# Attention and a routed FFN in one launch: routing counts ahead of the scores, weight halves and the last attention groups moved at the seam

## Reference

```python
qkv = xn @ w_attn.T                      # 16 heads of 16
# per batch row, in chunks of 128 tokens, q and k through elu(.) + 1:
scores = where(mask, q_c @ k_c.T, 0)
num = scores @ v_c + q_c @ S;  den = scores.sum(-1) + q_c @ z
S += k_c.T @ v_c;  z += k_c.sum(axis=chunk)
attn = (num / (den + 1e-6)) @ w_proj.T
# ffn: 8 experts of 256 -> 1024 -> 256, one per token
top = argmax(xn @ gate_w.T + gate_b + expert_bias)
ffn = relu(xn @ w1[top] + b1[top]) @ w2[top] + b2[top]
```

## Time and profile before

| | us |
|---|---|
| median of 3 runs | 522.24 |
| those runs | 522.82, 519.31, 522.24 |
| the profiled execution: its own time | 518.55 |
| its span, first to last instruction | 516.8 |
| TensorE, VectorE, ScalarE, GpSimd busy | 486.6, 397.0, 278.9, 303.5 |
| mean granted TensorE clock | 0.986 |

### The profile page before, as it was taken

How to read it: one execution, slowest core, us unless ns; L and a number is a source line. 1 busy time by engine, 2 the same in 40 slices (tenths; PEclk the granted TensorE clock), 3 DMA queues, 4 the chain that set the end, 5 groups by cost and what they waited for, 6 DMA issues and landing times.

```text
span 516.8 us, 17902 instructions
## 1 busy us (share of the span) xinstructions
PE 486.6 (94%) x6265; PEld 402.2 (78%) x6265; DVE 397.0 (77%) x851; ACT 278.9 (54%) x536; POOL 303.5 (59%) x498
## 2 busy tenths in 40 slices
PE   7699999999999999999977869999999999999996
PEld 6578887888878887888865658888888888888884
DVE  3678898988889888897889537777776776776775
ACT  3447888788787787877763313323323333333330
POOL 5666889879888888888753273344344344343122
PEclk9989999999999999999997989999999999999999
DMA  8715667686676676766530462221222222200000
GB/s 258 248 53 146 203 196 212 189 237 193 185 224 182 210 208 197 211 189 194 173 128 22 153 171 76 64 78 59 69 68 66 77 63 63 70 23 27 22 17 1
DMA packets 39059, 67.50 MB, mean 131 GB/s; under 512 B 6237, under 2 KB 14686, under 8 KB 38848
## 3 DMA queue, kind: packets, MB, share of 16 engines
q1 hardware_dynamic: 33840, 53.37, 33.5%
q0 software_dynamic: 5136, 12.99, 8.4%
HBM read 51.39 MB, written 17.69 MB: 134 GB/s over the span
## 4 chain that ended last, share of the span: by engine, by line
PE 85%; DVE 5%; issue 4%; POOL 2%; DMA 2%; ACT 1%; DVEq 0%; POOLq 0%; ACTq 0%
PE ps L682 20%; PE ps L695 19%; PE ps L424 8%; PE ps L466 6%; PE ps L495 6%; PE ps L539 5%; PE ps L479 5%; PE ps L442 4%; PE ps L509 3%; PE ps L525 3%; PE ps L647 2%; PE ps L449 1%; PE ps L531 1%; PE ps L407 1%; DVE AR L785 1%
## 5 line engine op out<-in xcount | busy, mean ns | idle before, releaser
L682 PEld LDWEIGHTS ps<-AR,W 128*128 x1872 | 131.2, 98 | 41.1 <-issue 2.0
L682 PE MATMUL ps<-AR,W 128*128 128x128 f16 x1872 | 155.8, 220 | 0.9 <-ACT AR L1264 0.9
L695 PE MATMUL ps<-W,ST 128*128 x624 | 151.4, 328 | 0.0
L1273 ACT ACTIVATE ST<-ST 128x512 f16<-128x512 f32 x78 | 49.2, 630 | 117.1 <-DVE ST L1080 117.1
L1080 DVE SCALAR_TENSOR_TENSOR ST<-ps,TAs,B1S 128x512 f32<-128x512 f32 x78 | 58.6, 751 | 48.5 <-PE ps L682 48.4
L1433 POOL DMA_INDIRECT out<-AR x39 | 39.6, 1015 | 94.7 <-DVE AR L1112 90.8
L1370 POOL TENSOR_TENSOR W<-ST,W 128x512 f16<-128x512 f32 x64 | 74.3, 1161 | 19.2 <-ACT W L1199 18.3
L785 DVE TENSOR_TENSOR AR<-ps,CT 128x512 f32<-128x512 f32 x128 | 81.9, 683 | 2.4 <-PE ps L466 2.2
L1428 POOL DMA_INDIRECT XR<-scr,AR x39 | 44.4, 1139 | 48.7 <-DVE AR L1100 25.4
L1092 DVE SCALAR_TENSOR_TENSOR ST<-ST 128x512 f16<-128x512 f32 x78 | 53.6, 687 | 14.9 <-ACT ST L1273 14.9
L424 PE MATMUL ps<-xT,WA 128*128 128x128 f16 x768 | 49.1, 221 | 3.4 <-ACT xT L1148 3.4
(11 more groups left out here) (149 smaller groups left out, 789.9 us busy)
## 6 DMA issues: line engine op xcount, KB each, us to landing
ST<-in_w SPq DMA_DIRECT2D x128, 256.0 KB, 4.4
scr<-XR SPq DMA_DIRECT2D x32, 256.0 KB, 2.2
XR<-in_x SPq DMA_DIRECT2D x32, 128.0 KB, 4.7
scr<-XR SPq DMA_DIRECT2D x32, 128.0 KB, 4.6
AR<-in_b SPq DMA_DIRECT2D x1, 1024.0 KB, 5.2
AR<-in_wall SPq DMA_DIRECT2D x2, 388.0 KB, 3.9
XR<-scr,AR POOLq DMA_INDIRECT x40, 3.6
out<-AR POOLq DMA_INDIRECT x39, 2.5
```

The lines of the kernel that those rows point to most:

```text
L682: a = e.matmul(dst, W[:, off:off + 57472][:, bass.ds(place_of(s), 128)], XT16[s % 2][:, xl * 256 + k * 128:xl * 256 + (k + 1) * 128], star ...
L695: a = e.matmul(PS[4 + s % 2][:, 0:w], src[h % 4][:, fs], W[:, off:off + 57344 + w][:, bass.ds(place_of(s), w)], start=(f == 0 and w == 512 ...
L1273: e.activation(HH[h % 4], H32[h % 2], ACT.Relu).then_inc(a_hh, 1)
```

## The change

Six edits at the seam; nothing is computed otherwise. A new semaphore v_kt marks that first_slots has written KT.

1. TensorE: place(3) goes ahead of scores(30).
2. GpSimd: km(31), and with it all w_lo behind it, waits for v_kt. w_lo(63) goes ahead of gather_x16(0).
3. VectorE: the three ids operations and the whole computation of the slots' experts go ahead of s_mask(30); to_slots(1) no longer waits for a count of its own engine; res(30) goes ahead of y(31).
4. ScalarE: seven splits in one piece ahead of y1(30).
5. TensorE: yt2(30), pr(30) and yt1(31) go into slot 0 (behind tx(0), steps 0 and 1); yt2(31) and pr(31) move from steps 3 and 5 to 4 and 6.
6. VectorE: res(31) goes behind low(0). ScalarE: y2(31) goes behind tx(1).

```diff
@@ -293,8 +293,8 @@
         v_mx, t_mx, v_mm, t_mxa, v_sc, v_ffn = (sem(n) for n in ("v_mx", "t_mx", "v_mm", "t_mxa", "v_sc", "v_ffn"))
 
         p_tt, p_carry, v_ro, p_pl = (sem(n) for n in ("p_tt", "p_carry", "v_ro", "p_pl"))
-        v_o16, v_ox, t_rk, v_own, v_es, v_eq, v_ao, t_ids, v_ids, d_c16 = (
-            sem(n) for n in ("v_o16", "v_ox", "t_rk", "v_own", "v_es", "v_eq", "v_ao", "t_ids", "v_ids", "d_c16"))
+        v_o16, v_ox, t_rk, v_own, v_es, v_kt, v_eq, v_ao, t_ids, v_ids, d_c16 = (
+            sem(n) for n in ("v_o16", "v_ox", "t_rk", "v_own", "v_es", "v_kt", "v_eq", "v_ao", "t_ids", "v_ids", "d_c16"))
 
         v_rb, t_tx, a_tx, v_out, t_g2 = (sem(f"f_{n}") for n in ("rb", "ptx", "tx", "out", "g2"))
 
@@ -609,9 +609,9 @@
                     e.transpose(PBX, BM[:, :], ID32).then_inc(t_bmx, 1)
 
 
+            place(3)
             scores(NC - 2)
             st(NC - 2)
-            place(3)
             inter(NC - 2)
             warm(70)
 
@@ -631,9 +631,6 @@
             e.wait_ge(S["t32"], n_state(NC - 2))
             inter(NC - 1)
             pv(NC - 1)
-            yt2(NC - 2)
-            pr(NC - 2)
-            yt1(NC - 1)
 
             def tx(s):
 
@@ -702,6 +699,7 @@
             e.wait_ge(v_es, 1)
             expert(0)
             tx(0)
+            yt2(NC - 2)
             for t in range(8 * NS + LAG):
                 s, f = t // 8, t % 8
                 if s < NS:
@@ -710,9 +708,13 @@
                         tx(s + 1)
                     if f == 4 and s + 1 < NS:
                         expert(s + 1)
-                if t == 3:
+                if t == 0:
+                    pr(NC - 2)
+                if t == 1:
+                    yt1(NC - 1)
+                if t == 4:
                     yt2(NC - 1)
-                if t == 5:
+                if t == 6:
                     pr(NC - 1)
                 if t >= LAG:
                     g2((t - LAG) // 8, (t - LAG) % 8)
@@ -974,12 +976,12 @@
                 e.tensor_reduce(OB, RB8, X_AX, ALU.add).then_inc(dv.up(), 1)
                 e.wait_ge(dv.sem, dv.n)
                 e.wait_ge(p_pl, 3)
-                e.tensor_tensor(KT, KS, OB, ALU.add).then_inc(dv.up(), 1)
+                e.tensor_tensor(KT, KS, OB, ALU.add).then_inc(v_kt, 1)
+                e.wait_ge(v_kt, 1)
 
             def to_slots(i):
 
                 c = slice(16 * i, 16 * i + 16)
-                e.wait_ge(dv.sem, dv.n)
                 e.tensor_tensor(EQS[:, :, c], SLX[:, :, c], bm(KT[:, c], NS), ALU.is_equal).then_inc(dv.up(), 1)
                 e.wait_ge(dv.sem, dv.n)
                 e.tensor_tensor(EQS[:, :, c], EQS[:, :, c], bm(IDX[:, c], NS), ALU.mult).then_inc(v_eq, 1)
@@ -1030,8 +1032,11 @@
             to_slots(1)
             places(2)
             places(3)
-            s_mask(NC - 2, 0)
-            s_mask(NC - 2, 1)
+            e.tensor_tensor(GE, bc(cc(C_SL, 5 * NP), 7), bm(CSF[:, 0:7], 5 * NP), ALU.is_ge).then_inc(dv.up(), 1)
+            e.wait_ge(dv.sem, dv.n)
+            e.tensor_reduce(ESF, GE, X_AX, ALU.add).then_inc(dv.up(), 1)
+            e.wait_ge(dv.sem, dv.n)
+            e.tensor_tensor(ESP, ESF, cc(C_PK, 5 * NP), ALU.mult).then_inc(dv.up(), 1)
             e.wait_ge(t_ids, 1)
             pid = PS[1][:, 0:NS]
             e.tensor_scalar(IDZ, pid, 0.0, 2048.0, ALU.is_equal, ALU.mult).then_inc(dv.up(), 1)
@@ -1039,29 +1044,25 @@
             e.scalar_tensor_tensor(IDP, pid, 0.0, IDZ, ALU.is_gt, ALU.subtract).then_inc(dv.up(), 1)
             e.wait_ge(dv.sem, dv.n)
             e.scalar_tensor_tensor(ids[:, :], pid, 2048.0, IDP, ALU.add, ALU.subtract).then_inc(v_ids, 1)
+            e.tensor_reduce(PKF, ESP.rearrange("p (j i) -> p j i", i=5), X_AX, ALU.add).then_inc(dv.up(), 1)
+            e.tensor_copy(es[:, :], ESF[:, 0:NS])
+            e.wait_ge(dv.sem, dv.n)
+            e.tensor_copy(pk[:, :], PKF).then_inc(v_es, 1)
+            s_mask(NC - 2, 0)
+            s_mask(NC - 2, 1)
             s_mask(NC - 2, 2)
             s_mask(NC - 2, 3)
             t32(NC - 2)
             y(NC - 3)
-            e.tensor_tensor(GE, bc(cc(C_SL, 5 * NP), 7), bm(CSF[:, 0:7], 5 * NP), ALU.is_ge).then_inc(dv.up(), 1)
-            e.wait_ge(dv.sem, dv.n)
-            e.tensor_reduce(ESF, GE, X_AX, ALU.add).then_inc(dv.up(), 1)
             s_mask(NC - 1, 0)
             s_mask(NC - 1, 1)
             s_mask(NC - 1, 2)
             s_mask(NC - 1, 3)
-            e.wait_ge(dv.sem, dv.n)
-            e.tensor_tensor(ESP, ESF, cc(C_PK, 5 * NP), ALU.mult).then_inc(dv.up(), 1)
             res(NC - 3)
-            e.wait_ge(dv.sem, dv.n)
-            e.tensor_reduce(PKF, ESP.rearrange("p (j i) -> p j i", i=5), X_AX, ALU.add).then_inc(dv.up(), 1)
-            e.tensor_copy(es[:, :], ESF[:, 0:NS])
             y(NC - 2)
-            e.wait_ge(dv.sem, dv.n)
-            e.tensor_copy(pk[:, :], PKF).then_inc(v_es, 1)
             scales_ffn()
+            res(NC - 2)
             y(NC - 1)
-            res(NC - 2)
 
             at = {}
 
@@ -1118,12 +1119,13 @@
                         e.wait_ge(v_es, 1)
                     expert(s)
                     bias(s, 0)
-                if s == 0:
-                    res(NC - 1)
                 if s >= 2:
                     add_up(s - 2)
                 if s < NS:
                     low(2 * s)
+                if s == 0:
+                    res(NC - 1)
+                if s < NS:
                     bias(s, 1)
                 if 1 <= s <= NS:
                     rest(s - 1)
@@ -1250,10 +1252,9 @@
             split(NW - 8, 1)
             vh(NC - 1)
             y1(NC - 3)
-            split(NW - 7, 4)
+            split(NW - 7, 7)
             y1(NC - 2)
             y2(NC - 3)
-            split(NW - 3, 3)
             y1(NC - 1)
             y2(NC - 2)
 
@@ -1273,10 +1274,11 @@
                 e.activation(HH[h % 4], H32[h % 2], ACT.Relu).then_inc(a_hh, 1)
 
             tx(0)
-            y2(NC - 1)
             for s in range(NS):
                 if s + 1 < NS:
                     tx(s + 1)
+                if s == 0:
+                    y2(NC - 1)
                 high(2 * s)
                 high(2 * s + 1)
 
@@ -1409,8 +1411,9 @@
 
             e.wait_ge(v_ox, 4)
             w_lo(NW - 8)
+            e.wait_ge(v_kt, 1)
             km(NC - 1)
-            for n in range(NW - 7, NW - 1):
+            for n in range(NW - 7, NW):
                 w_lo(n)
             e.wait_ge(S["xt"], NC)
             for c in range(NC - R, NC):
@@ -1434,9 +1437,7 @@
                                      bounds_check=NT - 1, oob_is_err=False).then_inc(d_sca[s % 3], 16)
 
             e.wait_ge(v_ids, 1)
-            gather_x16(0)
-            w_lo(NW - 1)
-            for s in range(1, NX0):
+            for s in range(NX0):
                 gather_x16(s)
             for c in range(NC - R, NC):
                 e.wait_ge(d_scr[c % R], 16 * (c // R + 1))
```

## The result

The changed kernel took 522.68 us in the median of 20 runs (520.92 to 526.56), the kernel before 520.79 (516.78 to 522.82) in as many beside it: a ratio of 1.0059 [1.0034, 1.0083], some 3.1 us slower; the medians alone differ by 1.9. That is within the 1% that was forecast as the likeliest outcome, and on its slower side; the forecast was +4.4 on a base of 520.8, so 525.2.

The account below looks back on a forecast made before the run. The prediction took the end to follow res(31), ahead of the hole before slot 3's transposes; +6.1 - 0.8 - 2.7 + 1.8 = +4.4 us on 520.8 gave 525.2 us (chance 0.42), range 516.0 to 529.0.

Parts of the forecast that it names:

- What bounds it: Where attention ends and slots begin: the end follows res(31) one to one, through its store and gathers to slot 3's transposes.
- Part 1: TensorE's place(3) ahead of scores(30): starts at 260.95 instead of 262.09, 1.14 us earlier for VectorE's chain.
- Part 2, what goes: VectorE ahead of KT: four 8-column operations blocked by GpSimd fall to some 0.2 each, 3.1 us saved.
- Part 2, what comes back: Behind KT: six GpSimd pieces go in front of seven VectorE operations, adding 6.8 us; places end at 274.8 against 272.30.
- VectorE keeps its turn: Rival: GpSimd gets in only where VectorE waits, two operations in front, places end at 270.2; 520.8 us, chance 0.23.
- 16-bit operations are not blocked: Rival: VectorE's seven operations behind KT are undisturbed, places end at 268.0; 518.1, at best 516.6 us; chance 0.20.
- Part 3: VectorE's pack of experts ahead of chunk 30's masks: these end at 281.35 instead of 275.27, 6.1 us late.
- What was to be given back up to pv(31): Between the masks of 31 and yt1(30): GE, ESP, PKF and casts no longer in between, 0.8 us back.
- fourth rival: TensorE's clock falls and stays at 1.2 GHz into slot 0: 3.5 us more on res(31), 528.7 us; chance 0.15.
- Part 4: ScalarE's seven splits hidden in idle time; gather_x16(0) issued by 279.0 instead of 282.52, landing ahead of pv(31)'s end.
- Part 5: Attention's last groups inside slot 0: slot 0 starts 2.7 us earlier after pv(31), res(31) gives back 1.8.
- The sum: On res(31), and so on the end: +6.1 - 0.8 - 2.7 + 1.8 = +4.4 us, giving 525.2 us.

Follow-up runs that it names:

- kernel with the ids wait: Kernel before with place(3) ahead of scores(30) and GpSimd's km(31) and low halves waiting for the ids (v_ids): 517.52 us, ratio 0.9964.
- combined kernel: Kernel before with GpSimd's km(31) and low halves behind the ids, place(3) first, and yt2(31), pr(31), res(31) moved earlier: 516.72 us, ratio 0.9943.
- the one with the 60 matmuls: Kernel before with extra matmuls in TensorE's gaps, 60 of them ahead of slot 3's transposes and 72 in three groups further up: 524.22 us, ratio 1.0094.

## Why the prediction was right, and where it was not

**What bounds it: right.** In all kernels without extra matmuls ahead of them and with pr(31) not moved up, the transposes of slot 3 follow res(31) at 10.9 to 11.4 us, and slot 0's earlier start alone gave nothing. It holds only down to a second limit, which the prediction didn't see: with res(31) earlier the distance is 12.0 to 12.1. This step decided the forecast: a reader who had taken "slot 0 starts 1.6 us sooner behind pv(31)" as a gain would have had the wrong sign.

**Part 1: right** in the trace (1.16 of 1.14 us); in the time it is undecided.

**Part 2, what goes: right.** Place to KT fell by 3.2 us (3.1 predicted).

**Part 2, what comes back: the mechanism right, the size off.** Six pieces of GpSimd did go in front of the seven operations, and the two rivals "VectorE keeps its turn" and "16-bit operations are not blocked" are refuted by the rows above and by the kernel with the ids wait. The term was mis-sized: 5.45 us instead of 6.8. I had charged the full 1.03 and 1.15 per piece; it came to 0.9. That the beginning of each piece overlaps the end of the VectorE operation ahead of it would fit, but isn't shown. The Trainium skill (SBUF — State Buffer, Who interferes with whom) had said full blocking without an exception for 16 bits; by that the trace agrees, at 1.2 to 1.65 us for what takes 0.48 to 0.69 alone.

**Part 3: right in kind, 0.9 us too much.** From the places to the end of the masks it took 5.67 us; the prediction had 6.55 (274.8 to 281.35), of which the operations blocked by w_lo(62) and (63) were again charged whole. The run without it puts the part at 2.9 us, the largest of the change.

**What was to be given back up to pv(31): failed in the profiled execution.** Instead of -0.8 from the masks to pv(31) it was +1.4. With the clock held up it was -0.75, as forecast; in the two runs without extra matmuls whose pack stands ahead of the masks it was 0.0 and -0.4. So the 2.15 us on top of the term are this execution's, and less in others. That is the fourth rival ("the clock falls and stays down") come true in part: it had set 3.5 us, and "decides once the masks of chunk 30 end after 280"; they ended at 277.94, and the clock was 0.53 from 270 to 280. That this was already 0.52 for a while before I had read; I had not asked what it would do to what comes next.

**Part 4: right.** The splits and gathers are not on the chain of waits to res(31); the gather behind w_lo(63) is issued at 276.25.

**Part 5: failed, and with its sign.** The prediction had -2.7 for slot 0's start and +1.8 for res(31), together -0.9. Measured from pv(31)'s end, res(31) came 1.6 us later (8.84 to 10.45); the time of the kernel with this part taken back has the same sign, 0.8 us by the ratios, undecided. Two terms: the start gained only 1.6, since TensorE takes 1.17 us of issue between pv(31) and its first transpose, for which the prediction had nothing (by the code it loads the registers of the experts there; in the old order 0.75 shows at the same place, behind yt1(31), and with 20 extra matmuls behind pv(31) 1.05 is still left; that the registers are the cause isn't shown), and since the transpose copy waits on an engine that has y2(30) first. And from slot 0's first product to res(31) it was 7.5 instead of 6.1: pr(30) took 2.02 at half clock and before, ahead of slot 0, 1.13:

```profile
285.13 1.13 PE L539 MATMUL ps<-AR 128*128 128x256 f32 x4 [0.62 <-ACT AR L1192]
```

That is 0.9 of the 1.4. The chain of waits also goes through y(31) on VectorE, 0.92 us from 294.95, which now stands between res(30) and bias(0, 0) and which my list left out. The three other runs with the new order have 7.2 to 7.3, each with a clock below full in slot 0's first microseconds, so no run shows what the order costs at full clock.

**The sum.** In the trace res(31) came 6.8 us later (32.15 to 38.97 in the table's count), not 4.4. The errors are -1.35 and -0.9 us (blocked pieces charged too high) against +2.5 (part 5) and +2.2 (from the masks to pv(31), mostly the clock), +2.4 net. The time moved by 3.1, 1.3 less than forecast. So the number was close by luck in part: terms of 1 to 2.5 us had opposite signs, and the traced execution is one of the slower ones.

**Still open:** how much of the 3.1 us the lower clock carries over all runs. Within one kernel the runs with the lower mean clock are the longer ones, yet raising the clock with extra matmuls gained nothing, so it may be partly a mark of something else. The changed kernel's eight runs at 0.979 and 0.980 have a median of 521.8 us, against 520.8 for the kernel before at that clock: 1.0 us apart.

## What to carry to other kernels

A block between two engines is not removed by a wait that moves one of them into the other's next chain: count the pieces beside each stretch on the way to the end, at some 0.9 us a piece here, and try them behind the last result of that chain, not in the middle. Before starting the next stage earlier, find the operation on which the stage's first hole hangs and ask what the new order puts in front of it, and count the time without any matmul at the stage's start (up to 1.36 us of issue ahead of slot 0's transposes here). A hole in TensorE's timeline while indirect DMAs run is not free space, so try a few extra matmuls in it before planning real work for it.

## What the runs showed of the hardware

**Turns are one for one.** Six pieces of GpSimd stretched six of the seven operations, five stretched five, and three stretched three (the changed kernel, the one with place and wait alone, the one without the wait), also where several of VectorE's were ready in a row, and also for 16-bit operands at 128x624 and 128x1024. GpSimd is stretched too: its low halves take 1.42 us each there (5.69 for four), against 1.23 before.

**TensorE's instructions arrive slowly while the gathers run.** Independent matmuls came at 4 to 6 per 0.73 us between 299.7 and 304, and real ones with gaps of 0.2 to 1.0 us in the combined kernel. The first gap lies 4 to 5 us behind the first gather's issue (291.8 and 296.6 in the combined kernel, 291.9 and 297.2 in the one with pr(31) early, 295.4 and 299.5 in the one with the 60 matmuls). That fetching the instructions shares its way with the gathers' transfers would explain it. The profile counts a single packet of the instruction queue beside 540 of the gathers in 296 to 308 of the combined kernel, and nothing ties it to the gaps, so this is argued and not shown.

**The mean granted clock varies from run to run of one kernel, and the time with it.** In the 102 runs of the kernel before beside the experiments (one of 2752.84 us left out), 34 had a mean clock of 0.9835 or more and a median of 517.7 us, 31 had about 0.980 and 520.8, 20 about 0.976 and 522.4, 7 about 0.970 and 524.1, and the other 10, below that, 525.3: some 4 us per 0.01 of clock. Of the changed kernel's 20 runs none was above 0.980; of the combined kernel's 12 eight were in the best group, at 516.1. Seen that way, a part of the 3.1 us is that the changed kernel has no runs in the group to which a third of the runs of before belong. What puts a run into its group stays open.
